# Part of one load of the last pass made early, into unused columns behind the thirteen slots' sums

## What is computed

```python
def block(x, w1, b1, gamma1, beta1, w2, b2, gamma2, beta2):
    identity = x
    out = conv3x3(x, quantize_weight(w1, 8), b1)
    out = relu(batchnorm(out, gamma1, beta1))
    out = conv3x3(out, quantize_weight(w2, 8), b2)
    out = batchnorm(out, gamma2, beta2)
    return relu(out + identity)

x = x + block(gn(x), ...)
```

## Time and profile before

| | us |
|---|---|
| median of three runs | 537.28 |
| the runs | 535.6, 537.28, 537.9 |
| span of the profiled execution | 535.1 |
| TensorE busy | 392.8 |
| VectorE busy | 462.4 |
| ScalarE busy | 331.4 |
| DMA in the last pass (stage 462.4 to 469.8) | 429 GB/s |

### The profile page before, as it was taken

How to read it: one execution, slowest core, us unless ns; L and a number is a source line. 1 busy time by engine, 2 the same in 40 slices (tenths; PEclk the granted TensorE clock), 3 DMA queues, 4 the chain that set the end, 5 groups by cost and what they waited for, 6 DMA issues and landing times.

```text
span 535.1 us, 20532 instructions
## 1 busy us (share of the span) xinstructions
PE 392.8 (73%) x9501; PEld 351.2 (66%) x9501; DVE 462.4 (86%) x593; ACT 331.4 (62%) x350; POOL 83.3 (16%) x147
## 2 busy tenths in 40 slices
PE   3999999999999999999999999999991000000000
PEld 1899889999999787899888998888880000000000
DVE  7999989999999757988988887798877999798995
ACT  3898799999999955765555566655515923544200
POOL 2027226666551500000000000000000000000000
PEclk9999999999999999999999999999996555555555
DMA  8934874433333000143333300000066999999997
GB/s 267 358 129 132 269 265 159 181 129 131 129 135 129 8 8 6 46 171 152 129 127 128 124 2 4 4 3 4 2 244 208 355 429 381 431 429 428 432 429 318
DMA packets 21965, 99.21 MB, mean 185 GB/s; under 512 B 6520, under 2 KB 8952, under 8 KB 16504
## 3 DMA queue, kind: packets, MB, share of 16 engines
q1 hardware_dynamic: 20256, 81.55, 40.4%
q10 hardware_dynamic: 1624, 16.36, 7.2%
HBM read 61.48 MB, written 35.50 MB: 181 GB/s over the span
## 4 chain that ended last, share of the span: by engine, by line
PE 72%; DMA 14%; DVE 10%; issue 2%; ACT 1%; SPq 0%; DVEq 0%
PE conv_ps L994 70%; DMA xa<-in_x_dram 11%; DVE slots L948 4%; DVE slots L951 3%; DMA out_dram<-xa 2%; DMA slots<-in_x_dram 1%; DVE xa L951 1%; DVE conv_ps L948 1%; PE conv_ps L957 1%; ACT split L435 0%; DVE gn_tup L674 0%; PE wt_ps L994 0%; PE stat_ps L994 0%; PE conv_ps L992 0%; DVE bn_tup L775 0%
## 5 line engine op out<-in xcount | busy, mean ns | idle before, releaser
L994 PE MATMUL conv_ps<-split,wmat 64*64 64x385 f16 (+3 forms) x9144 | 377.7, 324 | 2.1 <-ACT split L435 1.4
L994 PEld LDWEIGHTS conv_ps<-split,wmat 64*64 64x64 bf16 x9144 | 339.1, 107 | 37.6 <-issue 2.3
L469 ACT ACTIVATE slots<-conv_ps,par,evac_scale 128x784 f32<-128x784 f32 x124 | 123.7, 998 | 95.3 <-PE conv_ps L994 93.4
L775 DVE BATCH_NORM_STATS2 bn_tup<-slots 128x6 f32<-128x392 f32 x166 | 81.9, 555 | 15.6 <-ACT slots L469 15.6
L600 ACT ACTIVATE slots<-slots,skip_b,bn_w 128x3136 f32<-128x3136 f32 (+3 forms) x20 | 45.8, 2340 | 47.6 <-DVE slots L951 29.9
L674 DVE BATCH_NORM_STATS2 gn_tup<-slots 128x6 f32<-128x448 f32 x112 | 61.8, 612 | 0.9 <-DMA slots<-in_x_dram 0.9
L742 DVE TENSOR_TENSOR split<-slots,split 128x3136 f16<-128x3136 f32 (+4 forms) x36 | 57.2, 1607 | 3.5 <-ACT slots L449 0.9
L744 DVE SCALAR_TENSOR_TENSOR split<-slots,split 128x3248 f16<-128x3248 f32 (+3 forms) x18 | 53.6, 2979 | 2.3
L728 DVE TENSOR_SCALAR slots<-slots,bn_w 128x3248 f32<-128x3248 f32 (+3 forms) x18 | 30.4, 1688 | 21.4 <-ACT split L427 20.9
L427 ACT ACTIVATE split<-slots,bn_w 128x3248 f16<-128x3248 f32 x14 | 43.2, 3083 | 0.0
L477 ACT ACTIVATE xa<-conv_ps,par,evac_scale 128x784 bf16<-128x784 f32 x40 | 39.7, 994 | 0.0
(11 more groups left out here) (124 smaller groups left out, 214.4 us busy)
## 6 DMA issues: line engine op xcount, KB each, us to landing
out_dram<-slots SPq DMA_DIRECT2D x13, 1568.0 KB, 15.2
slots<-in_x_dram SPq DMA_DIRECT2D x51, 392.0 KB, 5.6
split<-in_x_dram ACTq DMA_DIRECT2D x5, 1568.0 KB, 23.4
slots<-in_x_dram SPq DMA_DIRECT2D x4, 1568.0 KB, 7.3
y_spill<-slots SPq DMA_DIRECT2D x3, 1624.0 KB, 7.3
slots<-y_spill SPq DMA_DIRECT2D x3, 1624.0 KB, 7.0
y_spill<-slots SPq DMA_DIRECT2D x3, 1568.0 KB, 5.8
slots<-y_spill SPq DMA_DIRECT2D x3, 1568.0 KB, 13.5
```

Source lines behind the costliest of these rows:

```text
L469: nc.scalar.activation(dst, src, ACT.Identity, bias=bias, scale=scale, accum_out=total).then_inc(evacuated[ph], 1)
L775: ins = nc.vector.bn_stats(bn_tup[:, 2 * (n - first) + s, :], rows[s])
L994: return nc.tensor.matmul(bank[:, r0:r1, w0:w1], lhs, rows[:, top + r0:top + r1, w0 + kx - 1:w1 + kx - 1], start=n == 0 and part is hi_all ...
```

## The change

Step 6 (IN_STRIPS) is cut in two parts, of EARLY = 13 x 112 = 1456 columns and of 1680. The x of the first part is loaded by SP, right after the load of step 0, into the 112 columns behind the pixels of all thirteen slots; ScalarE's load of step 6 brings only the other 1680. VectorE waits for both, sums the first part with its x read from the strips, and then the second. SP stores the two parts one after the other, and its last wait counts one store more.

```diff
     IN_PSUM = SPILL
+    STRIP = AREA - PIX
+    EARLY = RES * STRIP
+    IN_STRIPS = 6
     CUTS = [[0, CH, 2 * CH, 4 * CH, 6 * CH, PIX], [0, 4 * CH, PIX]] + [[0, PIX]] * (NP - 2)
+    CUTS[IN_STRIPS] = [0, EARLY, PIX]
...
+        strips_loaded = sem("strips_loaded")
...
+        def strips(ap):
+            return ap.rearrange("p (s m) -> p s m", s=RES)
...
             sp.dma_start(x3_buffers[0], pair_view(x, PAIR3[0])).then_inc(x3_loaded[0], 16)
+            sp.dma_start(slots[:, :, PIX:AREA], strips(pair_view(x, PAIR3[IN_STRIPS])[:, 0:EARLY])).then_inc(strips_loaded, 16)
             sp.wait_ge(round_done[1], NQ * (NP - 1))
...
-            sp.wait_ge(out_stored, 16 * (NP - 1 - SPILL))
+            sp.wait_ge(out_stored, 16 * sum(PARTS[SPILL + 1:]))
...
-                    sc.dma_start(x3_buffers[u % 4], pair_view(x, PAIR3[u])).then_inc(x3_loaded[u % 4], 16)
+                    first = EARLY if u == IN_STRIPS else 0
+                    sc.dma_start(x3_buffers[u % 4][:, first:PIX], pair_view(x, PAIR3[u])[:, first:PIX]).then_inc(x3_loaded[u % 4], 16)
...
                 dve.wait_ge(x3_loaded[u % 4], XCOUNT[u])
+                if u == IN_STRIPS:
+                    dve.wait_ge(strips_loaded, 16)
                 for k in range(PARTS[u]):
                     xs, y = part_of(x3_buffers[u % 4], u, k), sums_of(u, k)
+                    if (u, k) == (IN_STRIPS, 0):
+                        xs, y = slots[:, :, PIX:AREA], strips(y)
```

## The result

The changed kernel takes **533.16 us** (median of 12 executions, 532.52 to 536.17) against 537.4 of the kernel before on the same chip (12 executions, 535.6 to 538.75): a ratio of **0.9935, with a 95% interval of 0.9921 to 0.9949**. It is 3.5 us faster by the ratio; the forecast was 3.0.

A forecast was written before the change was run, and what follows sets the result against it. DMA was taken as saturated from 424 to about 527 us, then a hole of some 1.6 us. Bytes (1.74 us) plus the closed hole made 3.0: 537.3 - 3.0 = 534.3 us, range 532.8 to 537.0.

The forecast's parts named there:

- Part 1: Saturated last pass: step 6's load shrinks by 1456 of 3136 columns, so step 7's load starts 1.74 us sooner.
- Part 2: Strips' load on SP behind step 0's load, about 388.8: 2 to 4 us of DMA time, hidden in idle time.
- third rival: Strips hold SP's queue from 388.8, up to 25 us, delaying loads 1 and 2: 5 us slower; chance 0.07.
- Part 3: Step 6 summed in halves on VectorE: 7.28 instead of 6.91 us, ending before step 7's load lands, so no cost.
- Part 4: Step 6's two stores pair off by packet with loads 9 and 10: loads run 3.75 us ahead, closing the last-store hole.
- first rival: Only the bytes count: queues share by bytes or both store parts take one turn; hole stays, gain 1.7 us; chance 0.24.
- second rival: SP's queue leaves turns freed between 430 and 442 unused; step 3's stores land as before, gain 0; chance 0.08.
- step 7's load still starts at 449.9: Sign that the prediction is wrong; it forecast this load's issue near 448.1 instead of 449.87.
- what ScalarE's queue leaves is used at once: Within the bytes term: SP's queue takes the freed DMA time, so step 3's stores land 1.74 us sooner.

The follow-up runs named there:

- e2: The changed kernel, but step 6's result stored as one whole store after both parts are summed; early load stays: 535.39 us, ratio 0.9968 to the kernel before.
- e9: The changed kernel with early load and one whole store of step 6, a second time: 535.75 us, ratio 0.9968 to the kernel before.
- e1: The changed kernel once more, no edit, for a second profile: 534.43 us, ratio 0.9949 to the kernel before.
- e8: The changed kernel, but the strips' load issued inside the last pass, behind step 2's store: 536.79 us, ratio 0.9993 to the kernel before.
- e10: The changed kernel a third time, no edit: 534.59 us, ratio 0.9958 to the kernel before.
- e4: The kernel before, but step 9's load issued as two, of 1456 and 1680 columns; stores whole: 537.84 us, ratio 1.0014.
- e3: The kernel before, with step 6 summed and stored in two parts, its load whole, no early load: 536.15 us, ratio 0.9983.
- e6: The changed kernel with step 7 summed and stored in two parts as well: 534.59 us, ratio 0.9958 to the kernel before.
- e12: The kernel before, with step 3's result stored once in whole rows instead of five stores, nothing else: 535.91 us, ratio 0.9981.

## Why the prediction was right, step by step

**Part 1, the bytes: right in mechanism, and in size as far as the times tell.** 1.74 us were forecast; e2 and e9 give 1.7 by their ratios (intervals from 0.6 to 2.8 and 0.9 to 2.5). In e1 VectorE's wait at step 7 fell to 1.60, forecast 1.5, and load 7 was issued at 448.82, forecast 448.1 and a start of the pass 0.35 later. e8 shows the other side: the same load where DMA is full brings nothing that the times can tell. But in the first profile of the change, in e10, e2 and e9 step 7's wait fell by 0.6 us at most or not at all; see the last paragraph of this section.

**Part 2, the early load: right.** It was to take 2 to 4 us of DMA time and to land before 403. The strips landed at 398.6, the stage to 424 kept its share (0.81 against 0.82), and the idle stretch from 399.6 to 402.4 now has a share of 0.31, so 0.87 us of work have moved into it of the 2.8 that there were. The third rival is out: its decisive point was 9 us for the strips, and they held each engine for 2.2 (104 pieces, 21 ns apart, e8) to 2.6 us (25 ns each by their records); load 1 behind them landed at 402.3 instead of 399.6. The rule on pieces below 512 bytes (the Trainium skill, "DMA: Bandwidth & Descriptors", Specifications) gave an estimate of 3.5 us: these runs show 1.3 to 1.5 times the bytes' time and not twice.

The prediction's range for the strips, 1.74 to 25 us, could have been far narrower. The trace of the kernel before does have small pieces: the halo copies' 224 bytes took 16 ns each, and 12 loaded pieces of 256 bytes took 18 ns, so it is not quite so that it has no load in pieces below 512 bytes.

What the prediction put no price on is SP itself: 0.86 us for the issue of 1664 pieces, and 1.86 instead of 0.33 for the next. It was hidden, as the prediction said of a late issue there: SP's next wait came later.

**Part 3, the sum in two parts: right.** In e1 the parts of step 6 take 1.73 + 1.67 + 1.96 + 1.91 = 7.27 us (forecast 7.28) and end 1.6 us before load 7 lands.

**Part 4, the queues: right, and it is the term that makes the difference** between 1.7 and about 3. Turns go by packet: 277 against 277 with 3.07 against 1.86 MB, and the mirror e4 shifts the bytes the other way. The loads came 5.5 and 6.0 us after the one before (5.49 and 5.76 forecast), load 15 at 518.0 (517.1, with the pass 0.35 later and load 7 0.7 later), the last four stores 3.7 apart. The Trainium skill ("DMA: Bandwidth & Descriptors", Queues, rings and completion order) lets a packet hold typically 9 to 17 descriptors: here each turn is one row piece (load pieces 0.685 us apart in e1), and the first rival did not come.

**The sum.** The pass of e1 is 3.1 us shorter than before, forecast 2.6 to 3.3. The parts alone give 1.7 (e2, e9) and 0.9 (e3, by its ratio) or 1.3 (by its pass), the whole 2.3 to 3.5. No more can be told: one kernel's executions spread over 4 us. (In the prediction's chances two terms are exchanged: the second rival, time as before, is the 0.08 and belongs to "same", the third, slower, is the 0.07. Nothing else hangs on it.)

**What the prediction did not see** is that a single profile need not show part 1 at all. It named a sign of being wrong: that step 7's load still starts at 449.9. In two of the three profiles of the change it started later still, at 450.79 and 451.35. The step "what ScalarE's queue leaves is used at once" holds for most of the 16 engines and not always for the last one, on which everything waits. The last store out of xa lands in 16 parts, one for each engine; from the trace's record of the last 16 parts that landed, in us after the first sum of the pass:

```
kernel                 ninth part   last part
before                 41.49        41.68
e3, no early load      41.51        41.88
change, first          40.11        42.39
change, e1             40.02        40.29
change, e10            39.98        42.67
bytes alone, e2        40.05        42.20
bytes alone, e9        40.11        41.57
step 7 cut too, e6     39.90        40.02
```

In all six profiles that have the whole early load ahead of the pass and step 3's store in five, the ninth part landed 1.4 to 1.6 us sooner than before, near the 1.74 that were forecast. The last part did so in e1 and e6 alone. In the other four the last three parts came 0.5 us one behind the other, the time of eight 1568-byte pieces, as if one engine were some 2 us behind the rest; the last section has more on it.

## What to carry to other kernels

Where two queues shared saturated DMA engines here, they took turns by row piece, so the queue with the shorter pieces gave bytes away: cut a transfer on the queue that can wait, rather than on the one whose landing feeds the next issue. Bytes leave a saturated stretch only if they go to a place where DMA stands still, and a part of a load will do, if a corner of SBUF is free that long; a hole in front of the last transfer is closed by letting the work ahead of it run early. When one step of a pass is changed, compare passes and not spans, and take two profiles, one at least of an execution near the median.

## What the runs showed of the hardware

**The 16 engines do not end together, and by how much differs among executions of one kernel.** A transfer has landed when the last of its 16 parts has. For step 4's store, the first after the spilled sums' reload, the first, the fifteenth and the last part (from the trace's record of each part), with the pass:

```
kernel               first    15th     last   apart   pass
before               459.69   462.02   462.21   2.5   126.55
change, first        457.06   458.42   463.41   6.4   125.60
change, e1           458.69   460.15   460.44   1.7   123.44
change, e10          456.85   460.12   464.40   7.5   126.64
bytes alone, e2      457.83   459.97   463.63   5.8   126.54
bytes alone, e9      456.36   459.86   460.80   4.4   125.75
change, step 3 whole 456.28   458.16   458.36   2.1   122.18
```

Of the three profiles of the change the one with its engines closest together is 2 to 3 us shorter. Where they are far apart it is mostly one engine: in the first profile 15 parts land within 1.4 us and the last one 5.0 us later. In these three the distance stays while loads and stores fill the engines (6.4 us in the first profile up to the store landed at 512.0) and falls when the loads are over (3.6 at 522.8); in e2 it shrinks sooner, to 4.4 at 486.1. It begins early: in e10 step 1's store, issued at 424.10, already has its parts 2.9 us apart, in the first profile the reload issued at 424.68 has 1.8. In the five runs with 4.4 us or more (the first, e2, e9, e10 and e12) there are pieces between 424 and 446 us that took at least 0.5 us longer than others of their size, 2.1 to 5.0 us in sum, in e10 one of 6272 bytes that took 2.79 us instead of 0.239; in the nine others these sum to 1.1 us at most. The trace does not tell on which engine a piece ran, so that such a piece puts the last engine behind is likely and not shown. Near 450, 12.5 KB pieces took up to 1.4 us and more instead of 0.469 in the first profile and in e1 alike, so those do not tell the two apart. Why in some executions and not in others, no run here tells. That step 3's store in whole rows left the engines 2.1 and 2.5 apart both times, but 6.8 in e12, speaks against taking it for the cure.

**A row piece costs a fixed time and its bytes.** On one engine 12544 bytes took 469 ns, 6720 took 255, 5824 took 222, 1568 took 66, 448 took 25, 224 (the halo copies of the kernel before) took 16 and the 4 bytes of a semaphore 9. All seven lie within 1 ns of 8 ns + bytes / 27.2 GB/s, worked out from these rows; no step is to be seen at 512 bytes. The records of pieces that follow each other overlap by a few ns, so in a row they cost a little less: 21 ns for 448 bytes (e8).
